# Layer 0's preparation moved into the score banks, one step of each batch left without any, and the split of the maxima handed from VectorE to GpSimd

## The reference

```
q = (layernorm(x) @ Wq.T)  -> 32 maps of size 4      k = (ctx @ Wk.T) -> 32 maps       v = (ctx @ Wv.T) -> 16 heads of 8
a1, a2 = softmax(q1 k1) v, softmax(q2 k2) v
attn   = a1 - lam * a2 ; rms-normalised over the 8 features of a head
x      = x + tanh(g) * (attn @ Wp.T + bp)
x      = x + tanh(g) * experts(layernorm(x))
```

## Time and profile before

| | |
|---|---|
| three runs | 2429.80, 2433.78, 2422.18 us; median 2429.8 |
| profiled execution | 2424.42 us, its span 2422.6 us, mean granted clock 0.949 |
| PE | busy 2235.1 us, 92% |
| DVE | busy 1720.9 us, 71% |
| ACT | busy 1484.6 us, 61% |
| POOL | busy 1247.5 us, 51% |
| exponents, L1012 | 1152, 916 ns each |
| search reductions, L1070 | 1023 + 513, 672 ns each |

### The profile page before, as it was taken

The page is one execution under the profiler, slowest core; times in us unless marked ns, Lnnn a source line. Parts: engine busy times, 40 slices in busy tenths (PEclk is TensorE's granted clock), DMA queues, the critical chain, the costliest instruction groups (busy, mean ns, idle before and its releaser), DMA issues. The chain is left out here.

```text
span 2422.6 us, 67012 instructions
## 1 busy us (share of the span) xinstructions
PE 2235.1 (92%) x27256; PEld 1258.2 (52%) x27256; DVE 1720.9 (71%) x3761; ACT 1484.6 (61%) x2101; POOL 1247.5 (51%) x1322
## 2 busy tenths in 40 slices
PE   3899999999999999999996986999999999999798
PEld 2344444444444444444444763566666655666576
DVE  3778888888888888888872554766777766775544
ACT  3167777777777777777774432566777666767322
POOL 5234545545455454454523344666777666773232
PEclk9589999999999999999997996899999999999799
DMA  3624343443444434434311006666676675762100
GB/s 108 128 71 103 88 92 103 87 105 85 99 103 93 92 98 92 104 85 94 91 13 51 23 29 135 125 133 130 141 142 137 136 137 122 142 136 41 53 1 15
DMA packets 113419, 227.80 MB, mean 94 GB/s; under 512 B 46052, under 2 KB 58596, under 8 KB 112612
## 3 DMA queue, kind: packets, MB, share of 16 engines
q1 hardware_dynamic: 113124, 223.67, 41.8%
HBM read 146.77 MB, written 76.48 MB: 92 GB/s over the span
## 5 line engine op out<-in xcount | busy, mean ns | idle before, releaser
L1012 ACT ACTIVATE probs<-score_ps 125x896 f32<-125x896 f32 x1152 | 1014.1, 916 | 368.9 <-PE score_ps L911 368.0
L1070 DVE TENSOR_REDUCE max_part<-max_ps 112x1 f32<-112x500 f32 x1023 | 665.4, 672 | 129.9 <-PE max_ps L890 89.9
L927 PE MATMUL acc_ps<-probs,vext 125*32 125x224 f32 (+1 forms) x12288 | 680.5, 317 | 4.3 <-issue 3.6
L890 PE MATMUL max_ps<-kstack,qstack 48*112 48x500 f16 x1534 | 512.3, 407 | 23.8 <-ACT kstack L987 11.1
L1067 DVE CUSTOM_DVE_ANT_0 kstack<-max_ps,kstack 112x500 f32<-112x500 f32 x511 | 335.3, 675 | 142.2 <-PE max_ps L890 83.4
L927 PEld LDWEIGHTS acc_ps<-probs,vext 125*32 125x32 f32 x12288 | 258.7, 109 | 272.9 <-issue 266.3
L1070 DVE TENSOR_REDUCE max_part<-spare_ps 112x1 f32<-112x500 f32 x513 | 344.8, 672 | 78.2 <-PE max_ps L890 45.6
L911 PE MATMUL score_ps<-qstack,kstack 50*125 50x224 f16 (+1 forms) x6144 | 389.8, 244 | 4.3 <-ACT probs L1012 2.1
L911 PEld LDWEIGHTS score_ps<-qstack,kstack 50*125 50x125 f16 x6144 | 306.4, 135 | 154.2 <-issue 122.4
L890 PE MATMUL spare_ps<-kstack,qstack 48*112 48x500 f16 x770 | 312.4, 406 | 30.0 <-issue 16.7
L767 POOL CAST khl<-kstack 128x500 f16<-128x500 f32 x189 | 113.6, 601 | 350.4 <-ACT kstack L994 194.1
(11 more groups left out here) (203 smaller groups left out, 2621.8 us busy)
## 6 DMA issues: line engine op xcount, KB each, us to landing
kstack<-k_parts SPq DMA_DIRECT2D x384, 187.5 KB, 6.6
k_parts<-khl SPq DMA_DIRECT2D x128, 375.0 KB, 2.8
ctx_f<-in_ctx SPq DMA_DIRECT2D x32, 750.0 KB
ctx_f<-context_parts SPq DMA_DIRECT2D x32, 750.0 KB, 4.5
context_parts<-ctx_f SPq DMA_DIRECT2D x16, 750.0 KB, 3.4
context_parts<-kstack SPq DMA_DIRECT2D x16, 750.0 KB, 3.3
mask_in<-in_mask SPq DMA_DIRECT2D x128, 82.0 KB
qrows<-q_parts SPq DMA_DIRECT2D x384, 7.0 KB, 7.4
```

The source lines that it names most:

```text
L890: nc.tensor.matmul(room(("P", n, p))[0:PIECE, 0:TK], qstack[n % SLOTS][rows, c, PIECE * i:PIECE * (i + 1)], kstack[n % SLOTS][rows, c, TK ...
L927: last = nc.tensor.matmul(acc_ps[32 * j:32 * j + 32, TT * S * i:TT * S * (i + 1)].rearrange("p (s c) -> p s c", s=S), vext[n % SLOTS][:, t ...
L1012: nc.scalar.activation(probs[t % 2][:, 896 * h:896 * h + 896].rearrange("k (b c) -> k b c", b=2), score_ps[(t * H + h) % 2][0:KT, :, 0:448 ...
L1070: nc.vector.reduce_max(best, scores, AX.X).then_inc(s_red, 1)
```

## The change

In layer 0 a preparation no longer takes a turn in the three banks. The list `in_scores` gives each to a step, and `room` puts it into the score buffer whose exponent is taken first in that step: bank 0 of it for T, K, V and F, bank 1 for M and A. So TensorE waits before the preparation until that exponent is taken (`s_exp`, one exponent of the step). The halves alternate their order: the even steps compute half 0 first, the odd steps half 1 (`halves_of`), so that the buffer with the preparation is filled second in the next step. The first half of a step waits for both exponents of the step before; the second waits for the readout of that step's preparation.

The table `where` moves T, F and K one step later, leaves step 0 with none, puts M and V 0 together in step 7, and A and V 2 together in step 11. In step 0 both weigh groups stand between the two search pairs.

M is read out by ScalarE, scaled, into a piece of `mask_in2` that layer 0 doesn't use, and GpSimd splits it in three operations (`split_max`), placed behind the first third of the keys. Layer 1 keeps its order.

```diff
@@ the table of layer 0
-        where = {("T", 0): (0, 1), ("F", 0): (1, 1), ("T", 1): (2, 1), ("F", 1): (3, 1), ("T", 2): (4, 1), ("K", 0): (5, 1),
-                 ("V", 0): (6, 1), ("M", 0): (7, 1), ("K", 1): (8, 1), ("V", 1): (9, 1), ("K", 2): (10, 1), ("V", 2): (11, 1),
-                 ("A", 0): (11, 2)}
+        where = {("T", 0): (1, 1), ("F", 0): (2, 1), ("T", 1): (3, 1), ("F", 1): (4, 1), ("T", 2): (5, 1), ("K", 0): (6, 1),
+                 ("M", 0): (7, 1), ("V", 0): (7, 1), ("K", 1): (8, 1), ("V", 1): (9, 1), ("K", 2): (10, 1), ("A", 0): (11, 1),
+                 ("V", 2): (11, 1)}
@@ the order of the users, and their rooms
+            middle, last = at_step(n, t, 1), at_step(n, t, 2)
+            spare_uses += middle + last
+            if H == 2:
+                in_scores.update({user: n * NKT + t for user in middle})
+                middle = []
+            order += searched(n, t, 0) + middle + searched(n, t, 1) + last
+    def halves_of(step):
+        return (0, 1) if step % 2 == 0 or H == 1 else (1, 0)
     def room(user):
         if user in place_of:
             return rooms[place_of[user] % len(rooms)]
+        if user in in_scores:
+            return score_ps[halves_of(in_scores[user])[0]][:, int(user[0] in "MA"), :]
@@ TensorE, before a preparation
+                if user in in_scores:
+                    pe.wait_ge(s_exp, in_scores[user] * H + 1)
@@ TensorE, before the scores of a half
-            def scores(n, t, h):
-                number = (n * NKT + t) * H + h
-                at_least(pe, s_exp, number - 1)
+            def scores(n, t, place):
+                step = n * NKT + t
+                number = step * H + place
+                h = halves_of(step)[place]
+                if L.masked:
+                    at_least(pe, s_exp, number - 1)
+                elif place == 0:
+                    at_least(pe, s_exp, number)
+                else:
+                    at_least(pe, s_exp, number - 2)
+                    for user in in_scores:
+                        if in_scores[user] == step - 1:
+                            pe.wait_ge(*drained(user))
@@ TensorE, the step
+                    weighed = (n, t - 1) if t else (n - 1, LAST)
                     for i in range(2):
-                        if t:
-                            weigh(n, t - 1, i)
-                        elif n:
-                            weigh(n - 1, LAST, i)
-                        if i == 0:
+                        if i == 1 and (t or H == 1):
                             for user in at_step(n, t, 1):
                                 use(user)
                             search(searched(n, t, 1))
+                        if weighed[0] >= 0:
+                            weigh(*weighed, i)
+                    if t == 0 and H == 2:
+                        search(searched(n, t, 1))
@@ ScalarE reads M out
+                if kind == "M":
+                    at_least(act, s_mr, 3 * n)
+                    nc.scalar.activation(max_f, spare_ps[0:L.tiles, 0:PIECE], ACT.Copy, scale=1.0 / BIG).then_inc(s_mc, 1)
@@ GpSimd splits it
+            def split_max(n):
+                pool.wait_ge(s_mc, n + 1)
+                high, low = max_rows[0:L.tiles, 0, 0:PIECE], max_rows[0:L.tiles, 1, 0:PIECE]
+                nc.gpsimd.tensor_copy(high, max_f).then_inc(s_mr, 1)
+                pool.wait_ge(s_mr, 3 * n + 1)
+                nc.gpsimd.tensor_tensor(max_rest, max_f, high, ALU.subtract).then_inc(s_mr, 1)
+                pool.wait_ge(s_mr, 3 * n + 2)
+                nc.gpsimd.tensor_scalar(low, max_rest, BIG, None, ALU.mult).then_inc(s_mr, 1)
@@ GpSimd, each batch
                 if n + 3 < B:
-                    split_keys(n + 3)
+                    split_keys(n + 3, range(1))
+                if L is L0 and n + 1 < B:
+                    split_max(n + 1)
+                if n + 3 < B:
+                    split_keys(n + 3, range(1, NTHIRD))
```

More of the change, by code:

```diff
@@ L533, in attend @@
     s_mr = sem(L.name + "_max_split")
+    s_mc = s_mr if L.masked else sem(L.name + "_max_copied_out")
+    max_f, max_rest = (T["mask_in2"][0:L.tiles, 4 * PIECE * i:4 * PIECE * (i + 1)].bitcast(F32) for i in range(2))
     s_os = sem(L.name + "_output_copied")
@@ L980, in drain @@
                 kind, n, i = user
-                if kind == "M":
+                if kind == "M" and L.masked:
                     return
```

31 lines of the change are left out of this document (18 added, 13 removed).

## The result

The changed kernel takes 2364.87 us (median of 4 runs, 2354.94 to 2366.89), the kernel before 2425.99 on the same chip: ratio 0.9746 with the interval 0.9727 to 0.9765. It is faster by 61 us; 39 to 43 were forecast. Its profiled execution took 2366.89 us, span 2365.1.

A forecast was written before the change was run, and what follows sets the result against it. TensorE in V steps, elsewhere three banks shared by five users, bound the kernel. 2424.4 - 51.5 (28 batches, 1.84 less) + 9.0 (end of layer 0) = 2381.9, plus 5.4: 2387 us; own range 2374 to 2402, wide 2360 to 2420.

The forecast's parts named there:

- rival C: Before preparations: the exponent is over in time, T and F steps 2.69, 49 us less, 2338 (half: 2362); chance 0.12.
- The wait for a bank: Second search piece's 0.16 wait for VectorE: goes in all steps with a preparation; TensorE-only lengths T/F 2.69, K 2.92, V 3.02.
- The new wait: Before each preparation TensorE waits for the first exponent: start at 1.42, not 1.26, behind scores; 0.16 more in 11 steps.
- Rival A: Before preparations: TensorE restarts late, the new wait costs as much as the old; 40 us more, 2427, no change; chance 0.13.
- K 3.08 and V 3.18: Lengths in us of steps with a K or V preparation: TensorE-only 2.92 and 3.02, plus 0.16 for the new wait.
- M 0.26: In the step where M stands ahead of V 0: M adds 0.26 us a batch.
- A 0.07: In the step where A stands ahead of V 2: A adds 0.07 us, what step 11 has over 3.02.
- Step 0 at 2.23: First step of a batch: waiting for both exponents makes it 2.23 us, against TensorE work of 2.12.
- The end of layer 0: Last 17 steps, without search: the wait for both exponents makes 1.70 into 2.23, 9.0 us more.
- The second wait of the scores: Second half of the scores waits for the preparation's readout: 0.4 us to spare, costed at nothing.
- Rival D (the clock): More short TensorE gaps make the clock fall: 100 us at half clock cost up to 100, 2440 and above; chance 0.03.
- rival B: Rows of maxima land 2.8 us late for the next batch's scores: 81 us more, 2468; chance 0.06.

The follow-up runs named there:

- two-and-one run: Kernel before with its three banks split, search pieces alternating in two and all preparations in the third: 2508.86 us, ratio 1.0353.
- the wait alone in the kernel before: Kernel before, with TensorE also waiting for the step's first exponent before each preparation of layer 0: 2445.49 us, ratio 1.0092.
- three dense orders: Changed kernel with both weigh groups side by side in TensorE's step, in three different orders: 2414.42, 2470.07 and 2405.82 us.
- the run with the rotation back: Changed kernel, but the score halves change order only behind a step with a preparation; elsewhere the first half awaits one exponent: 2354.61 us, ratio 0.9725.
- the old table: Changed kernel with the table `where` and the order of step 0 as in the kernel before: 2414.38 us, ratio 0.9945.
- packed early: Changed kernel with TensorE's step as both score halves, search pair, both weigh groups, search pair, preparation: 2470.07 us, ratio 1.0199.
- packed: Changed kernel with TensorE's step as scores half, search pair, second scores half, both weigh groups, search pair, preparation: 2414.42 us, ratio 0.9949.

## Why the prediction was right, point by point

The mechanism is right and its size too small. 2364.87 us lies below the forecast's own range of 2374 to 2402, and 5 us inside the wide one of 2360 to 2420, whose lower part was there for rival C. Rival C didn't come; what carried the time there are terms that were charged too high and the offset between one run and the median. That the wide range held is in so far luck.

- **The wait for a bank goes from all steps with a preparation: right.** No search piece behind a preparation waits for VectorE; T and F steps are 2.83 to 2.89 (2.85 forecast). The two-and-one run shows that this hangs on the third bank. (The prediction says that the trace agrees on this; but the trace of before shows only the wait, and that it ends is shown by the changed kernel.)
- **The new wait costs 0.16: right,** 1.42 behind the scores in the trace, in every kind of step. Rival A (restart as dear as before) and rival C (exponent over in time) fall by this row. The restart of 0.05 holds where the weight load carries the wait; where an instruction of its own in front of the load carries it, it is up to 0.14, as the wait alone in the kernel before and the three dense orders show.
- **K 3.08 and V 3.18: 0.06 too long.** The term that failed is the pair behind a preparation, for which 0.41 was taken from the earlier trace rows. It is 0.35 (739.68 to 740.03), the same as behind T. The row that was taken, behind V, has 0.48 for its two pieces where T's has 0.42: a piece was a little late there too. So the reading that a V step has no wait for VectorE and is TensorE alone was wrong by this 0.06. Measured are 3.02 and 3.12, 0.24 less a batch. VectorE's timeline of that V step in the kernel before shows the wait: the reduction that frees the second piece's bank ends at 741.74, and with 0.05 for the restart the piece starts at 741.79, 0.06 behind the first.

```profile
740.48 1.26 DVE L1070 TENSOR_REDUCE max_part<-max_ps 112x1 f32<-112x500 f32 x2 [0.16 <-PE max_ps L890]
```

- **M 0.26: mis-sized, 0.10** (741.96 to 742.06). The 0.26 is the duration of the record, and the next matmul starts before it ends. V behind it takes 0.79 (742.06 to 742.85) and not 0.84. With the pair's 0.06, M and V together take 3.17 and not 3.44. **A 0.07: mis-sized the other way, 0.19.** It was read where A stands at the end of a step, ahead of the scores; in front of V it costs what A and V have over V alone, 3.31 against 3.12, so that step took 3.31 and not 3.25.
- **Step 0 at 2.23: right to the hundredth.** Its TensorE work was put at 2.12 with the weigh groups apart; in a row they make it 1.89 (721.21 to 723.10 in the run with the rotation back), but the wait for both exponents hides this. Steps 0 and 1 together are 5.12; VectorE doesn't bind in the changed kernel, but it does as soon as step 0 gets shorter.
- **Sum of a batch:** 35.59 forecast, 35.18 measured; 0.18 of it from K, 0.06 from V 1, 0.27 from M with V 0, against 0.06 for A with V 2 and 0.03 for the T and F steps. In 28 batches this is 11.5 us.
- **The end of layer 0: +9.0 forecast, +6.15 measured.** The last four copies of the accumulators lie 33.20, 26.73 and 21.62 apart before, and 32.43, 29.07 and 26.20 after: 0.8 less, 2.3 and 4.6 more. For the last of them twelve steps of 0.53, 6.4, were charged; but a batch of 21.62 has steps of 1.80 on average, not 1.70, and batch 29 still gains.
- **The second wait of the scores at nothing: right in the changed order, by some 0.26 us only.** The 0.4 to spare lies there in the records (readout over at 740.38, second half at 740.78), but TensorE needs 0.14 of it to go on, where 0.05 was taken. Three orders and the old table used it up, and each time it became the bound.
- **GpSimd's maxima: right.** 0.27, 0.39 and 0.48 us for the three operations; issue over at 32.2 (31.7 forecast); rival B didn't come, and VectorE's relief changed nothing.
- **Rival D (the clock):** didn't come. The granted clock is 1.00 from 155 to 1200 us, the full 2.4 GHz, with 11 waits of 0.16 us more in a batch. The Trainium skill warns of a clock that swings between its levels with small idle times between matmul groups that cycle through banks (TensorE: Matmul & The Clock Gate, section A second HAM failure mode: psum-queue depth-cycling); this trace shows no such swing.
- **The median:** 5.4 us were added because the profiled execution of before lay under its runs' median. With more runs that median is 2425.99, 1.6 above, and after's profiled run lies 2.0 above its own. Of the 22 us between forecast and result, 15 are the trace's and 7 this offset. A spread of over 10 us between single runs should not be carried over as if it belonged to one of them.

What stays open: why the time behind layer 0 differs by up to 20 us between profiled runs whose code there is the same (from the last copy-out to the end 1132.2 us in the changed kernel, 1124.6 with the rotation, 1120.8 in packed early, 1140.3 with the old table). So no difference of a few microseconds between two kernels is read from their times alone here.

## What to carry to other kernels

Count buffers by how many pieces are in flight, not by who uses them: taking one user out of a shared set helped because the others then had all three banks, while giving each user its own bank made the kernel slower. A readout that is late holds up whoever uses its bank next, in either set of banks; look for the step in which it is late (here step 0, behind the accumulators' copy) and clear it. And before packing an engine's work denser, add up the ring through the other engine's readout and back; if its length is near the step's, the packing only moves idle time.

## What the runs showed of the hardware

- The two weigh groups in a row take 0.90 us and apart 0.52 each, start to start (721.75 to 722.65 in the changed kernel; 737.35 to 737.87 and 739.12 to 739.63 in the kernel before): 0.14 less in a row.
- A pair of search matmuls takes 0.31 to 0.35 us for both, since the two start at the same instant; when one waits, the pair takes up to 0.82, as in the two-and-one run.
- From a K preparation's start to the first matmul that may reuse its bank, ScalarE's readout of 128x500 in between, pass 1.57 to 1.58 us in three kernels; the readout itself is 0.59 of it.
- TensorE goes on 0.05 us behind the end of the exponent when its weight load carries the wait (changed kernel: 738.89 to 738.94), and 0.10 to 0.14 behind the releaser when that wait is a semaphore instruction in front of the load (the wait alone in the kernel before: 0.10 with K, and 748.81 to 748.95 with V; packed: readout over at 741.37, scores at 741.52). Where a matmul has two waits it matters which of them the load carries; that swapping them gains the difference was not tried.
